# Places of the rope chain's steps, of the wide output projection, and the order of the opening in a four-layer transformer kernel

## Chip, cores, metric

One core of one Trainium2 chip. The metric is the device time of one execution in microseconds (us). The kernel before took 4762.24 us (median of 3 runs, 4760.87 to 4765.71). "TensorE" (PE, with its weight loads PEld), "VectorE" (DVE), "ScalarE" (ACT), "GpSimd" (POOL) and "SyncE" (SP, which issues the DMAs) are the five engines; each takes its instructions in order.

## The reference, cut to what matters

Four different transformer layers are applied to `x` (2 batches, 1024 tokens, 256 channels), each with modulated layer norms, self-attention, cross-attention to a context of 77 tokens and an MLP:

```python
def _rope(x, sin, cos):                 # layer 2 alone, on q and k
    xe = x[..., ::2]; xo = x[..., 1::2]
    re = xe * c - xo * s
    ro = xe * s + xo * c
...
mod = cond @ W + b                      # per layer; shifts and scales of its three norms
h = _ln(x) * (1 + scale) + shift        # layer 0 and 1: silu(cond)
q, k, v = h @ Wq, h @ Wk, h @ Wv
x = x + softmax(q @ k.T * s) @ v @ Wo + bo       # self
x = x + softmax(q @ kc.T * s) @ vc @ Wo + bo     # cross, keys and values from the context
x = x + gelu(h @ W1 + b1) @ W2 + b2
```

Layers 0 and 1 have 16 heads of 16 channels ("narrow"), layers 2 and 3 have 16 heads of 64 ("wide"). Layer 2 rotates q and k (rope), layer 3 does not; otherwise their attention is the same.

## The kernel before

The program is one list `order` of steps (L569 to L836). A `Plan` (L571) gives each step a place, a number on a scale of attention units, and sorts them; `put(lo, hi, steps)` spreads several steps evenly from lo to hi. All five engine programs (`tensor_program` L936, `scalar_program` L1306, `vector_program` L1500, `gpsimd_program` L1892, `sync_program` L1974) walk the same list and issue what the step has for them. So a step's place sets where its instructions stand in every engine's queue, and an instruction that waits on a semaphore holds up all that is behind it on its engine. Between stages there is a step "rest", a barrier of all engines. The products of TensorE go to PSUM buffers that a ring hands out in turn (`take`); a buffer is free again once its reader has signalled.

**Wide self-attention** (one stage for both batches): 32 units, each 512 queries of 2 heads against 1024 keys in 8 key tiles. For every key tile TensorE computes two scores (L948), ScalarE the exponentials (L1390), TensorE the weighted values (L1128). The row maxima for a later unit come before it: TensorE L1020, VectorE's reduction L1667 (8 per unit). GpSimd sums the probabilities of key tiles 1 to 5 (L1957, L1961), VectorE adds 6 and 7 (L1741), TensorE sums over partitions (L1138), VectorE takes reciprocals (L1756) and scales, TensorE projects (L1170), VectorE adds to x (L1777). Score banks let TensorE be two scores ahead of ScalarE's exponentials.

Every 4 units a new group g of 4 heads is prepared ("natural tiles", place o = 4g - 4 and later): weights are loaded and split, values computed (v64), and q and k each in two halves of 512 tokens (nat64). In layer 2 such a half is a **rope chain**: TensorE's projection into a pair of banks (12 matmuls, L948), ScalarE's copy (L1356), VectorE's product with cosine (L1652, frees the bank pair) and GpSimd's with sine (L1935), GpSimd's two rotations (L1941, L1942), ScalarE's copy rounded to the high part (L1362), VectorE's subtraction for the low part (L1659). It is planned in three steps, `nat64`, `rturn`, `rlow`; ScalarE's L1362 belongs to `rturn`, right behind GpSimd's rotation. Then SyncE stacks the tiles by DMA (`kstack`, `qstack`: 8 DMAs each, L2093 and L2110), for which it waits for the chain's end. Layer 3 has a copy (L1344) and a subtraction (L1639) only. The cosine product lies in the tile of the weight stage, the sine product in that of the normalised layer-norm input.

**Wide cross-attention**: 32 units with 77 keys. For each: scores twice (cs, L948), maxima (L1724), exponentials (L1411), reciprocal (L1733), GpSimd's scaling (L1948), transposes (cturn, L1052) and ScalarE's copy (L1419), weighted values (cav, L1064), ScalarE's output copy (fin, L1400), projection (proj, L1170), addition (L1777). Their places (L604 to L609) relative to the unit: -1.25, -0.85, -0.45, 0, 0.5, 0.51, 0.9.

**Opening**: the small loads and x, statistics of the first layer norm (L1543 to L1551), then `cond` for all four layers: 12, 12, 8 and 12 products of 4 matmuls with two columns (L948), ScalarE's eviction (L1316) and VectorE's combination into scale and shift (L1518 to L1527). Then the norm in four rounds: L1558, transposes L969, scale and shift L1329, split L1569 and L1571; the addition of a bias row to x (GpSimd, L1899); the split of the first weights (L1581, L1905); a barrier. The first stage then begins with the projections of batch 0 (L948), their storing and restacking by DMA, and 32 maxima (L1024, L1671) before the first scores.

## Time and profile before

| | |
|---|---|
| median of 3 runs | 4762.24 us |
| the profiled execution, its own time | 4768.35 us |
| its span, first to last instruction | 4766.6 us |
| busy share PE, DVE, ACT, POOL | 87%, 65%, 44%, 28% |
| mean granted TensorE clock | 0.935 of full |

The span is a little less than the execution's time, which is more than the median of the runs by 6 us. Places in the trace: opening 0 to 77 us, layer 2 self-attention 1771 to 2839, its cross-attention to about 3220, layer 3's self-attention to 4308, its cross-attention to about 4610. A busy share is that of an engine over all stages; a line such as `ACT x <- POOL y: us, times, longest` says how long ScalarE stood before its instructions of line x until those of line y had ended.

### The profile page before, as it was taken

What the parts mean: (1) busy time and instruction counts of PE and PEld (TensorE: products, weight loads), DVE (VectorE), ACT (ScalarE), POOL (GpSimd) and SP (SyncE); (2) the same over time, 40 slices, a digit from 0 to 9 for tenths busy, and PEclk for the clock granted to TensorE, in tenths of its full rate; (3) what the DMA queues carried; (4) which work ended last, traced back from release to release, by engine and by line L of the source; (5) the groups of instructions that cost most, each with busy time, mean ns of one, the idle gap of its engine ahead of it and who ended that gap; (6) DMA issues with size and microseconds to landing.
All of it is one profiled execution on the core that took longest, in us unless ns stands there. A gap on an engine that the chain in (4) does not pass through costs nothing. (4 is left out here: it accounts for less than half of the span.)

```text
span 4766.6 us, 56541 instructions
## 1 busy us (share of the span) xinstructions
PE 4157.7 (87%) x20828; PEld 2548.7 (53%) x20828; DVE 3079.0 (65%) x4625; ACT 2080.2 (44%) x3756; POOL 1344.8 (28%) x664
## 2 busy tenths in 40 slices
PE   6899989789998878888888876788799899997989
PEld 4343356633335665554555445567555555545768
DVE  4888855688885655667666763345477777774455
ACT  2555544355554433333333434454244444444541
POOL 1000001200001024554555553321144444451120
PEclk9999989899998988999999998889899999998999
DMA  4223231122323142222222215333223233215420
GB/s 120 29 53 47 42 56 34 45 27 52 45 42 59 32 79 65 46 52 63 56 62 62 50 29 120 80 63 73 62 61 72 54 70 76 63 39 135 104 64 18
DMA packets 158515, 286.64 MB, mean 60 GB/s; under 512 B 36458, under 2 KB 70052, under 8 KB 157216
## 3 DMA queue, kind: packets, MB, share of 16 engines
q1 hardware_dynamic: 158240, 283.03, 28.6%
q8 instruction: 166, 2.72, 0.3%
q14 instruction: 109, 0.89, 0.1%
HBM read 105.01 MB, written 29.64 MB: 28 GB/s over the span
## 5 line engine op out<-in xcount | busy, mean ns | idle before, releaser
L948 PE MATMUL PS<-t 128*128 128x512 f32 (+4 forms) x7896 | 2006.1, 386 | 224.1 <-ACT t L1390 100.9
L948 PEld LDWEIGHTS PS<-t 128*128 128x128 f32 (+2 forms) x7896 | 1258.7, 188 | 786.0 <-issue 259.5
L1390 ACT ACTIVATE t<-PS 128x512 f32<-128x512 f32 (+2 forms) x1600 | 1164.7, 750 | 1094.6 <-PE PS L948 1088.1
L1667 DVE TENSOR_REDUCE t<-PS 128x1 fp32r<-128x1024 f32 x512 | 621.9, 1220 | 311.8 <-PE PS L1020 305.6
L1128 PE MATMUL PS<-t 128*32 128x512 f32 (+2 forms) x4352 | 816.9, 615 | 0.2
L1671 DVE TENSOR_REDUCE t<-PS 128x1 f32<-128x512 f32 x1024 | 649.2, 682 | 75.5 <-PE PS L1024 74.1
L1961 POOL TENSOR_TENSOR t<-t 128x1024 f32<-128x1024 f32 x256 | 621.1, 2426 | 148.1 <-ACT t L1390 123.6
L1024 PE MATMUL PS<-t 96*128 96x512 bf16 x1024 | 374.9, 396 | 37.5 <-DVE t L1671 13.5
L1020 PE MATMUL PS<-t 128*128 128x512 f32 x1024 | 340.4, 416 | 59.2 <-DMA t<-t 26.8
L1957 POOL TENSOR_TENSOR t<-t 128x1024 f32<-128x1024 f32 x64 | 155.6, 2431 | 747.7 <-PE PS L1138 469.7
L1899 POOL TENSOR_TENSOR t<-t 128x2048 f32<-128x2048 f32 x24 | 109.6, 4569 | 899.2 <-DMA t<-in_rows 560.6
L1128 PEld LDWEIGHTS PS<-t 128*32 128x32 f32 (+2 forms) x4352 | 171.7, 122 | 331.3 <-issue 326.9
L1170 PE MATMUL PS<-t 128*128 128x256 f32 x1024 | 284.3, 427 | 69.7 <-ACT t L1400 51.1
L1024 PEld LDWEIGHTS PS<-t 96*128 96x128 bf16 x1024 | 97.0, 97 | 375.7 <-DVE t L1671 157.1
L1170 PEld LDWEIGHTS PS<-t 128*128 128x128 f32 x1024 | 211.5, 213 | 119.5 <-ACT t L1400 63.8
L1777 DVE TENSOR_TENSOR t<-PS,t 128x1024 f32<-128x1024 f32 x128 | 156.6, 1223 | 169.8 <-PE PS L1170 169.6
L1020 PEld LDWEIGHTS PS<-t 128*128 128x128 f32 x1024 | 198.0, 198 | 125.5 <-DVE t L1667 32.4
L1756 DVE RECIPROCAL PS<-PS 128x256 f32<-128x256 f32 x128 | 224.7, 1756 | 12.5 <-PE PS L1138 12.5
L1258 PE MATMUL PS<-t 128*128 128x256 f32 x1536 | 215.9, 292 | 13.4 <-DVE t L1873 4.7
L1258 PEld LDWEIGHTS PS<-t 128*128 128x128 f32 x1536 | 204.8, 197 | 26.0 <-issue 10.1
L1411 ACT ACTIVATE t<-PS,t 128x77 f32<-128x77 f32 x512 | 159.3, 324 | 105.9 <-DVE t L1724 105.8
L1873 DVE TENSOR_TENSOR t<-t 128x512 fp32r<-128x512 f32 x128 | 112.8, 882 | 128.2 <-ACT t L1493 127.0
(134 smaller groups left out, 3936.2 us busy)
## 6 DMA issues: line engine op xcount, KB each, us to landing
t<-t SPq DMA_DIRECT2D x512, 128.0 KB, 3.6
t<-t SPq DMA_DIRECT2D x256, 256.0 KB, 3.9
t<-scr_n SPq DMA_DIRECT2D x288, 128.0 KB, 6.3
scr_n<-t SPq DMA_DIRECT2D x72, 256.0 KB, 2.2
t<-t SPq DMA_DIRECT2D x256, 64.0 KB, 2.0
t<-in_L_Wg SPq DMA_DIRECT2D x16, 768.0 KB, 4.5
t<-in_L_W SPq DMA_DIRECT2D x36, 256.0 KB, 3.3
t<-in_L_Wo SPq DMA_DIRECT2D x64, 128.0 KB, 2.6
```

What stands on the lines that cost most here:

```text
L948: ins = e.matmul(out, l, r, start=i == 0, stop=i == len(terms) - 1, tile_position=tp)
L1020: ins = e.matmul(o[:, 512 * h:512 * h + 512], u.smq[j][qt], u.smk[j][h], start=True, stop=True)
L1024: e.matmul(o, u.smq[j][qt], u.smk[j][half], start=True, stop=True).then_inc(*bank_full[k].inc(nth))
L1128: ins = e.matmul(banks[S.ot][wd * j:wd * j + wd, :], u.v[j][kt], P[0:S.pr, j, :], start=kt == 0, stop=kt == S.nkt - 1, tile_position=(0, w ...
L1170: ins = e.matmul(o[:, 256 * q:256 * q + 256], S.OR[n % 2][:, 128 * q:128 * q + 128], u.wo[:, :], start=True, stop=True)
L1258: ins = e.matmul(banks[4 + q][:, 0:D], l, r, start=m == 0 and t == 0, stop=m == 7 and t == 2)
L1390: e.activation(dst, src, ACT.Exp, scale=S.L.scale).then_inc(*expd.inc((S.i, i)))
L1411: ins = e.activation(S.PQ[n % 3][:, j, t, :], o[:, 256 * t + CT * b:256 * t + CT * b + CT], ACT.Exp, bias=S.NM[n % 3][:, at], accum_out=S. ...
L1667: e.tensor_reduce(S.MT[m % 2][:, qt, j:j + 1], o, AX.X, ALU.max, negate=True).then_inc(*bank_free[k].nth(nth))
L1671: e.tensor_reduce(S.NMX[:, 4 * j + qt, half:half + 1], o, AX.X, ALU.max).then_inc(*bank_free[k].nth(nth))
L1756: e.reciprocal(o[:, hs], o[:, hs]).then_inc(*recip_made.inc((S.i, n, h)))
L1961: e.tensor_tensor(S.AP_[:, :, :], S.AP_[:, :, :], P[1][:, :, :], ALU.add).then_inc(*pool_summed.inc((S.i, n, kt)))
```

## The change

1. The rope chain is planned in five steps instead of three: `nat64` (projection, ScalarE's copy), `rcos` (cosine on VectorE, sine on GpSimd), `rturn` (rotation on GpSimd), `rhigh` (ScalarE's high copy), `rlow`. A new function `nat64_chain` gives each its own place, in layer 2's self- and cross-attention. The first groups of both stages, in the MLP before and at the start of cross-attention, keep an evenly spaced list, now of five steps.
2. In both wide cross-attentions the projection stands at 1.3 instead of 0.9.
3. Opening: layer 0's modulation weights are loaded before x; the first weights are loaded and split before the norm; only layer 0's products come before the norm, layer 1's stand three at a time between its rounds; layer 2's come after the first projections, layer 3's between the maxima, and the bias addition at -7.5. The norm waits for its own layer's modulation alone.

```diff
@@
-        Wmod = [sbt(c, [128, 2, 128 * L.nmod]) for L in Ls]
+        Wmod = [sbt(c, [128, 2, 128 * L.nmod]) for L in Ls[1:]]
         mods = [sbt(c, [128, L.nmod, NB]) for L in Ls]
+        sbt(c, [128, 120])
+        Wmod.insert(0, sbt(c, [128, 2, 128 * Ls[0].nmod]))
@@
-                             (0.9, ("proj", S, u.n, 0))):
+                             (1.3, ("proj", S, u.n, 0))):
@@
-                out += [(w, S, g, qk, half) for w in ("rturn", "rlow")]
+                out += [(w, S, g, qk, half) for w in ("rcos", "rturn", "rhigh", "rlow")]
         return out
+
+    def nat64_chain(plan, S, g, qk, at, steps):
+
+        for half in range(2):
+            for i, what in enumerate(("nat64", "rcos", "rturn", "rhigh", "rlow") if S.L.rope else ("nat64",)):
+                plan.put(at[half] + steps[i], 0, [(what, S, g, qk, half)])
@@
-    order.append(("setup",))
     first = line[0]
-    norm0 = norm_steps(first)
-    order.extend(norm0[:9])
-    order.extend(("cond", L) for L in Ls)
-    order.extend(norm0[9:])
-    order.extend(weight_steps(first))
+    order.append(("setup", 0))
+    order.append(("mod_load", Ls[0]))
+    order.append(("setup", 1))
+    order.append(("w_load", first, 0))
+    order.append(("setup", 2))
+    order.extend(("mod_load", L) for L in Ls[1:])
+    order.extend(("ln_stats", first, t) for t in range(8))
+    order.append(("ln_rstd", first))
+    order.append(("w_split", first, 0, 0))
+    order.append(("cond", Ls[0], 0, 12))
+    order.extend(("ln_norm", first, t) for t in range(4))
+    for q in range(4):
+        order.append(("ln_turn", first, q))
+        order.append(("cond", Ls[1], 3 * q, 3 * q + 3))
+        order.append(("ln_split", first, q))
+        order.extend(("ln_norm", first, t) for t in range(2 * q + 4, min(2 * q + 6, 8)))
@@
                         begin16_steps(S, plan, -20, -19, -17, -9, -8)
+                        plan.put(-16, 0, [("cond", Ls[2], 0, 8)])
+                        plan.put(-9, -8, [("cond", Ls[3], 2 * i, 2 * i + 2) for i in range(6)])
+                        plan.put(-7.5, 0, [("ln_bias", first)])
@@
-                        plan.put(o + 2.3, o + 3.7, nat64_steps(S, g, 0))
+                        if L.rope:
+                            nat64_chain(plan, S, g, 0, (o + 1.3, o + 2.9), (0, 0.15, 0.3, 0.95, 1.1))
+                        else:
+                            plan.put(o + 2.3, o + 3.7, nat64_steps(S, g, 0))
@@
                         plan.put(o - 0.9, o - 0.9, [("w_split", pg, g % 4, int(g != 4))])
+                        if L.rope:
+                            plan.put(o + (0.1 if g != 4 else 0.45), o + (0.5 if g != 4 else 0.75),
+                                     [("v64", S, g, t) for t in range(2)])
+                            late = 0 if g != 4 else 0.3
+                            for qk, at in ((1, (0.35 + late, 0.8 + late * 0.8)), (0, (1.25 + late * 0.5, 1.65 + late * 0.2))):
+                                nat64_chain(plan, S, g, qk, [o + x for x in at], (0, 0.05, 0.1, 0.3, 0.34))
+                            continue
@@
-                w.wait_ge(mod_made, "all")
+                w.wait_ge(mod_made, (p.L.i, "all"))
@@
-            elif what == "rturn":
+            elif what == "rhigh":
                 S, g, qk, half = a
@@
-            elif what == "nat64":
+            elif what == "rcos":
                 S, g, qk, half = a
@@
-                e.dma_start(cols[:, :], A["cols"]).then_inc(*setup_in[0].inc(0, 16))
-                e.dma_start(cT[:, :, :], A["cT"]).then_inc(*setup_in[1].inc(0, 16))
-                e.dma_start(ident[:, :], A["ident"]).then_inc(*setup_in[2].inc(0, 16))
-                e.dma_start(sel[:, :], A["sel"]).then_inc(*setup_in[3].inc(0, 16))
+                part, = a
...
+                if not part:
+                    e.dma_start(cT[:, :, :], A["cT"]).then_inc(*setup_in[1].inc(0, 16))
+                    e.dma_start(cols[:, :], A["cols"]).then_inc(*setup_in[0].inc(0, 16))
+                elif part == 1:
+                    for h in range(2):
+                        e.dma_start(X[:, 4 * h:4 * h + 4, :], x[:, 4 * h:4 * h + 4, :]).then_inc(*x_in[h].inc(0, 16))
+                    e.dma_start(ident[:, :], A["ident"]).then_inc(*setup_in[2].inc(0, 16))
+                else:
+                    e.dma_start(sel[:, :], A["sel"]).then_inc(*setup_in[3].inc(0, 16))
+                    for h in range(2, 4):
+                        e.dma_start(X[:, 4 * h:4 * h + 4, :], x[:, 4 * h:4 * h + 4, :]).then_inc(*x_in[h].inc(0, 16))
```

## Rows read from the trace of the kernel before

**Rows 1.** Busy time by stretch: stretch, length, PE, PEld, DVE, ACT, POOL, PEclk, DMA.

```profile
1821.16:2738.98 917.82, 806.04 (x3348) 472.63 (x3347) 618.08 (x574) 351.17 (x561) 495.86 (x227) 0.94 0.25 55
3416.44:4208.20 791.76, 762.64 (x3348) 451.47 (x3347) 570.16 (x546) 326.84 (x533) 342.25 (x143) 0.99 0.28 63
2887.68:3212.02 324.34, 253.60 (x1276) 193.43 (x1276) 129.10 (x231) 166.75 (x604) 106.19 (x70) 0.87 0.38 83
4333.68:4602.19 268.51, 238.34 (x1276) 180.67 (x1276) 115.14 (x219) 154.98 (x592) 48.25 (x34) 0.93 0.49 105
```

**Rows 2.** TensorE's waits (us, times, longest) in 1821 to 2739, then 3416 to 4208.

```profile
PE PS L948 <- ACT t L1390: 82.0, 56, 6.8
...
PE PS L948 <- ACT t L1390: 12.2, 29, 2.2
```

**Rows 3.** ScalarE's waits in 1821 to 2739.

```profile
ACT t L1362 <- POOL t L1942: 141.9, 28, 7.0
```

**Rows 4.** Timeline, one rope chain, Q (start, duration, what, idle before).

```profile
2004.90 1.03 ACT L1356 ACTIVATE t<-PS 128x1024 f32<-128x1024 f32 x1 [4.15 <-PE PS L948]
...
2005.96 1.23 DVE L1652 TENSOR_TENSOR t<-PS,t 128x1024 f32<-128x1024 f32 x1 [1.61 <-ACT t L1356]
2006.01 2.38 POOL L1935 TENSOR_TENSOR t<-t 128x1024 f32<-128x1024 f32 x1 [2.67 <-ACT t L1356]
...
2011.90 1.26 POOL L1942 TENSOR_TENSOR t<-t 128x512 f32<-128x512 f32 x1
...
2013.19 1.06 ACT L1362 ACTIVATE t<-t 128x1024 fp32r<-128x1024 f32 x1 [6.28 <-POOL t L1942]
...
2014.79 2.07 PE L948 MATMUL PS<-t 128*128 128x512 f32 x4 [2.50 <-ACT t L1390]
```

**Rows 5.** VectorE's groups in 1821 to 2739 (busy us, mean ns).

```profile
L1659 DVE TENSOR_TENSOR t<-t 128x1024 fp32r<-128x1024 f32 x28 | 48.0, 1716 | 47.0 <-ACT t L1362 47.0
```

**Rows 6.** TensorE's waits in 2870 to 3300, layer 2's cross-attention.

```profile
PE PS L1170 <- ACT t L1400: 33.5, 15, 4.7
PE PS L1052 <- POOL t L1948: 29.9, 7, 8.4
```

**Rows 7.** Timeline, an undisturbed unit of layer 2's cross-attention.

```profile
3034.19 1.04 PE L1052 MATMUL PS<-t 128*77 128x128 f32 x8
...
3036.34 1.08 PE L1064 MATMUL PS<-t 77*64 77x512 f32 x4 [0.16 <-ACT t L1419]
...
3038.87 1.22 POOL L1948 TENSOR_TENSOR t<-t 128x616 f32<-128x616 f32 x1 [5.47 <-DVE t L1733]
3039.04 1.99 PE L1170 MATMUL PS<-t 128*128 128x256 f32 x8 [0.48 <-ACT t L1400]
...
3040.87 1.04 PE L1052 MATMUL PS<-t 128*77 128x128 f32 x8
```

**Rows 8.** Timeline of the opening.

```profile
6.73 0.43 DVE L1543 BATCH_NORM_STATS2 t<-t 128x6 f32<-128x256 f32 x1 [2.75 <-DMA t<-in_x]
...
11.30 0.21 ACT L1321 ACTIVATE t<-t 128x8 f32<-128x8 f32 x1 [6.89 <-DVE t L1549]
...
14.93 37.71 PE L948 MATMUL PS<-t 128*128 128x2 f32 x176 [14.93 <-DMA t<-in_Wmod]
...
35.91 0.17 DVE L1518 TENSOR_SCALAR t<-t 128x2 f32<-128x2 f32 x1 [9.30 <-ACT t L1316]
...
39.32 0.23 DVE L1527 TENSOR_SCALAR t<-t 128x2 f32<-128x2 f32 x1
...
69.25 2.61 DVE L1569 CAST t<-t 128x512 fp32r<-128x512 f32 x1 [2.32 <-ACT t L1329]
...
72.51 0.95 DVE L1581 CAST t<-t 128x1536 fp32r<-128x1536 f32 x1
...
77.33 15.22 PE L948 MATMUL PS<-t 128*128 128x512 f32 x60 [9.23 <-POOLq L1969]
```

**Rows 9.** Timeline, the first maxima of the first stage.

```profile
106.47 18.74 PE L1024 MATMUL PS<-t 96*128 96x512 bf16 x32 [6.03 <-DMA t<-scr_n]
```

More of the change, by code:

```diff
@@ L952, in tensor_program @@
             if what == "cond":
-                L, = a
+                L, lo, hi = a
                 w.wait_ge(wmod_in[L.i], L.i)
@@ L957, in tensor_program @@
                 src = sT if L.silu else cT
-                for m in range(L.nmod):
+                for m in range(lo, hi):
                     o, k, nth = take(w, ring, ("cond", L.i, m))
@@ L1308, in scalar_program @@
             if what == "setup":
+                if a[0]:
+                    continue
                 w.wait_ge(setup_in[1], 0)
@@ L1311, in scalar_program @@
             elif what == "cond":
-                L, = a
+                L, lo, hi = a
                 w.wait_ge(setup_in[0], 0)
-                for m in range(L.nmod):
+                for m in range(lo, hi):
                     o, k, nth = full(w, ("cond", L.i, m))
@@ L1502, in vector_program @@
             if what == "setup":
+                if not a[0]:
+                    e.memset(ones[:, :], 1.0).then_inc(*set_up.inc("ones"))
+                if a[0] < 2:
+                    continue
                 w.wait_ge(setup_in[2], 0)
                 e.tensor_copy(identb[:, :], ident[:, :]).then_inc(*set_up.inc("ident"))
-                e.memset(ones[:, :], 1.0).then_inc(*set_up.inc("ones"))
             elif what == "cond":
-                L, = a
+                L, lo, hi = a
+                if hi < L.nmod:
+                    continue
                 k, nth = where["cond", L.i, L.nmod - 1]
@@ L1520, in vector_program @@
                         if aff is None:
-                            e.tensor_copy(mb, mod[:, 2 * sh + k, :]).then_inc(*mod_made.inc("all"))
+                            e.tensor_copy(mb, mod[:, 2 * sh + k, :]).then_inc(*mod_made.inc((L.i, "all")))
                         else:
@@ L1526, in vector_program @@
                             w.wait_ge(mod_made, (L.i, s, k, 1))
-                            e.tensor_scalar(ma, ma, col(aff + "_w", k), None, ALU.mult).then_inc(*mod_made.inc("all"))
+                            e.tensor_scalar(ma, ma, col(aff + "_w", k), None, ALU.mult).then_inc(*mod_made.inc((L.i, "all")))
             elif what == "ln_stats":
@@ L1924, in gpsimd_program @@
                                     ).then_inc(*nat_2.inc((S.i, ch)))
-            elif what == "nat64" and a[0].L.rope:
+            elif what == "rcos":
                 S, g, qk, half = a
@@ L1981, in sync_program @@
             if what == "setup":
-                e.dma_start(cols[:, :], A["cols"]).then_inc(*setup_in[0].inc(0, 16))
-                e.dma_start(cT[:, :, :], A["cT"]).then_inc(*setup_in[1].inc(0, 16))
-                e.dma_start(ident[:, :], A["ident"]).then_inc(*setup_in[2].inc(0, 16))
-                e.dma_start(sel[:, :], A["sel"]).then_inc(*setup_in[3].inc(0, 16))
+                part, = a
                 x = A["x"].rearrange("(t p) d -> p t d", p=128)
-                for h in range(4):
-                    e.dma_start(X[:, 4 * h:4 * h + 4, :], x[:, 4 * h:4 * h + 4, :]).then_inc(*x_in[h].inc(0, 16))
-            elif what == "cond":
+                if not part:
[9 more added lines that the diff above has]
+                        e.dma_start(X[:, 4 * h:4 * h + 4, :], x[:, 4 * h:4 * h + 4, :]).then_inc(*x_in[h].inc(0, 16))
+            elif what == "mod_load":
                 L, = a
```

## The prediction

> **What bounds the kernel now.** I read the page first, then busy time by stretch, then who waits for whom, then the timeline of single chains. The profiled execution took 4768.35 us, which is the sum's base. No engine is saturated over the whole; TensorE is nearest, so the question is where it stands still. Layer 2 and layer 3 run the same wide attention, so layer 3 serves as a yardstick. From the first partial sum of unit 0 to that of unit 28 of self-attention, both stretches hold exactly 3348 TensorE matmuls; layer 2 needs 917.8 us and layer 3 791.8 us, at mean granted clocks of 0.94 and 0.99 [rows 1]. In the cross stretch (first to last scaling of probabilities) it is 324.3 against 268.5 us for 1276 matmuls each [rows 1]. Those two differences, 126.0 and 55.8 us, are what rope costs where TensorE should hide it.
>
> The waits say how. In layer 2's self stretch TensorE's score matmuls wait 82.0 us for ScalarE's exponentials, in layer 3's 12.2 us [rows 2]. ScalarE itself waits 141.9 us, 28 times, for GpSimd's second rotation instruction (L1942) ahead of the high copy L1362 [rows 3]. The timeline of one half chain shows it [rows 4]: ScalarE's copy from PSUM at 2004.90, the sine product on GpSimd for 2.38 us, the two rotations ending at 2013.16, the high copy at 2013.19, and only at 2014.79 TensorE's next scores, 2.50 us idle. ScalarE takes work in order; with two exponentials of look-ahead, a wait of 5 to 6 us passes through to TensorE.
>
> **Rope chains in self-attention.** Nothing is added or removed: 7 groups x Q, K x 2 halves = 28 chains keep all instructions. The high copy moves from the place of the rotation (0.09 unit after the projection for K, 0.12 for Q) to 0.3 unit after it, the subtraction L1659 to 0.34; cosine, sine and rotation get places at 0.05 and 0.1. Without the excess a unit lasts 791.8 / 28 = 28.3 us, so the high copy is due 8.5 us after the projection's place instead of 3. GpSimd's part, measured from the end of ScalarE's copy, is 2.38 + 2 x 1.26 = 4.9 us, with a partial sum between (as in this timeline) 7.2 us [rows 4]. It fits, so the 141.9 us should go almost entirely. What queues behind the moved places: on VectorE the cosine product frees the PSUM pair, and at most one maximum (eight per unit, 0.125 apart) can precede it; on GpSimd the fifth partial sum of a unit now comes after sine and rotation of the last Q half, some 1.3 us late for the sum that VectorE continues; on SyncE the stacking DMAs of Q start at 2.05 units of the group, the last subtraction is at 1.99, and eight K DMAs (from 2.01) are issued before them, so they don't start later. The next weight load is at 2.5. Upper bound: layer 3's pace, 126. I leave 16 us unrecovered (28 additional high copies that scores can meet, about 0.4 us each, and the late fifth sums): **110 us**. Lower bound 60, if half the wait only changes its place.
>
> One rule speaks against the new place. The row: the subtraction L1659 averages 1.716 us over 28 [rows 5] where an undisturbed VectorE pass over as many elements takes 1.23 [rows 4]; it sits beside GpSimd additions already. Put later, it falls amid GpSimd's partial sums (as long as the sine product, 2.38) oftener. The Trainium skill (SBUF — State Buffer, Who interferes with whom) says that a VectorE instruction with two SBUF inputs and a GpSimd one that reads SBUF exclude each other, the later one waiting it out whole. The trace's longer passes agree with it. I don't take a cost for this, since VectorE is busy 618 of 918 us there [rows 1]; what it would be if all of it told is rival (a).
>
> **Rope chains in cross-attention.** Six groups (12 half chains) move, in the same way. TensorE waits 29.9 us for the scaling L1948, queued behind sine and rotations, and 33.5 us at the projection for ScalarE's output copy, queued behind the high copy [rows 6]. After: the first half has the scaling between sine and rotation. From the end of the projection matmuls: copy 1.1, sine 2.4, scaling 1.2, so the probabilities' transposes can begin at 4.7; TensorE has 2.2 us of work until then (36.34 to 39.04 without 0.48 idle [rows 7]), a wait of 2.5, of which 0.6 is in every unit already (next part): 1.9. The second half comes 1.6 units later, and costs some 0.7. That leaves 2.6 us per group where the excess over layer 3 is 55.8 / 6 = 9.3: 6.7 x 5 = 33, and for the fifth group (g = 4) I add only 2. Its first projection now stands at 8.3 units, amid the layer norm that it needs (6.75 to 9.2), and its sine must wait for the norm's last split, since both share a tile. **35 us**; bounds 0 and 56.
>
> **Output projection 0.4 unit later.** Both wide cross stages. In an undisturbed unit TensorE goes transposes 3034.19, ..., projection 3039.04 (0.48 idle), next transposes 3040.87 [rows 7]: period 6.68, of which 0.16 + 0.48 = 0.64 waiting. Moved behind the second scores, the projection no longer waits for the output copy. But VectorE's addition of its result (1.23 us) now comes before the reciprocal that the scaling needs. From the projection's start: matmuls 1.99, addition 1.23, reciprocal and hand-over 0.3 (an estimate), scaling 1.22 = 4.7 us until the next transposes. Transposes and second scores take 1.99 (34.19 to 36.34 without 0.16), so TensorE's own work in that time is 6.68 - 0.64 - 1.99 = 4.05, and the period is 1.99 + 4.7 = 6.7. The wait changes its cause: **0 us**. Bounds: the 0.48 could go in the 32 units of one stage (+16), or a layer norm's VectorE work in the same gap could add 0.65 for half of 62 units (-20).
>
> **Opening.** Now all 176 modulation matmuls run from 14.93 for 37.71 us, 0.857 per product of four [rows 8]; then four rounds of norm, transposes and split until 72.51, the weight split, the first projection at 77.33 [rows 8]. After: layer 0's 12 products come first. Its weight DMA goes ahead of the x quarters (8 tiles, two quarters, are needed). About 3.1 MB arrived between 6.73, when the first quarter was there, and 14.93, 0.38 MB/us; so the second quarter lands at 6.73 + 1.57 / 0.38 + 0.52 / 0.38 = 12.2. Statistics take 4.4 (6.73 until ScalarE's root at 11.30, less the hand-over), so the root is at 16.6. ScalarE evicts products only behind the root and three banks hold three, so nine follow: 16.6 + 9 x 0.857 = 24.3, with the vector work 25.5. The rounds took 19.9 with 1.2 of vector work; with three layer-1 products in each, and layer 1's vectors (3.6, 35.91 to 39.55) before the last split, I take 20.6 (19.9 - 1.2 + 3.6, less 1.7, since the bias addition on GpSimd no longer stretches a cast of the last round, 2.61 [rows 8]; an estimate). First projection at 46.5: 30.8 earlier. The weight split leaves the path; the bias addition on GpSimd goes beside the maxima and is due only before the first output addition. Given back: layer 2's 8 products (6.9) lie in the gap before the first maxima at 106.47, their vectors, now before VectorE's memset, cost about 2 of their 3.6. Layer 3's 12 (10.3 us) stand among 32 maxima that take 18.74, 0.59 each at VectorE's pace [rows 9]: I charge 6; bounds 0, and 20.6 if all are exposed at TensorE's lower clock level. Net **23 us**, bounds 9 and 31.
>
> Layer 1's MLP holds the first chains of layer 2, now in five evenly spaced steps: 0, up to +5.
>
> **Sum:** 110 + 35 + 0 + 23 = 168; 4768.35 - 168 = 4600. The median of the shown runs, 4762.24, is 6 below the profiled one, so the forecast for the median is **4594 us**.
>
> **Rivals** (all for the median).
> (a) GpSimd and VectorE block each other: every later subtraction meets a partial sum, is lengthened by its 2.38 us, and passes that on to TensorE through the maxima behind it; 28 x 2.38 = 66, 168 - 66 = 102 gives 4660. For: 1.716 against 1.23 [rows 4, 5]. Against: VectorE has idle time. The rule of the Trainium skill above (SBUF — State Buffer) would have it so.
> (b) Layer 2 becomes as fast as layer 3 throughout, and the opening reaches its bound: 126 + 56 + 31 + 5 = 218, 4544. Against: GpSimd still has 28 x 4.9 us more to do.
> (c) The steps don't take effect: positions differ but ScalarE still meets an unfinished rotation (GpSimd delayed by partial sums), so only the opening stays: 4739.
> (d) Slower: VectorE's queue becomes the gate. The cosine product, behind whatever VectorE has first, holds one of two PSUM pairs, and the projection's addition stands before every reciprocal. If cosine comes more than 4.5 us (126 / 28) after the copy, self-attention loses what it won: at 5.2 us, 20 slower; in cross 64 x 1.23 - 35 = 44 slower; opening 23 faster: 4803.
> (e) As (c), with the opening's gain lost to layer 3's products: 4760.
>
> **How the numbers follow.** Forecast 0.60, (a) 0.22, (b) 0.08, (c) 0.05, (d) 0.03, (e) 0.02. The forecast's own spread is about 4560 to 4640 (self 80 to 126, cross 15 to 45, opening 15 to 28); the range has to reach (a): 4555 to 4670, leaving out (c), (d), (e) and most of (b). A measurement of this kernel can tell about 0.2% (9.5 us) from no change. Faster: 0.60 + 0.22 + 0.08 + 0.05 = 0.95; same 0.02; slower 0.03.
>
> **What would show it.** In the profile after: ScalarE's wait for L1942's successor near zero; TensorE's wait for exponentials in layer 2's self stretch near 20 us, its clock near 0.99, and 28 units in about 808 us; cross 324 down to about 290, with short waits at the transposes instead of the projection; layer 3's cross unchanged at 268; first projection near 46, first maximum 23 to 30 us earlier than 106.47. The prediction is wrong if ScalarE still waits over 50 us there, if VectorE's cosine product lets TensorE wait for a bank, or if layer 3's cross moves by more than 16 us.

## The result, and the profile after

The changed kernel takes 4627.17 us (median of four runs, 4616.11 to 4631.79) against 4761.56 us of the kernel before (four runs, 4753.2 to 4765.71): ratio 0.9717, 95% interval 0.9695 to 0.9739. The forecast was 4594, with a range of 4555 to 4670. The profiled execution took 4616.11 us, the fastest of its four, so the profiles differ by 152.2 us and the medians by 134.4. What the profiles differ by can be laid out along the program, by the same instructions in both: 21.7 us in the opening, 5.8 in layers 0 and 1 up to layer 1's last transposes of maxima, -9.5 from there to layer 2's first transposes, 88.5 in the 28 units of layer 2's self-attention, 45.0 in its cross stretch, -3.8 in layer 3's cross stretch, and 4.5 in all that is left. The forecast had 23, 0, 0, 110, 35, 0, 0. (A minus sign means slower.) The 5.8 are chance: in the ten profiles taken with this opening and layer 1 unaltered, layer 1's last transposes stand anywhere from 1570.6 (this one) to 1579.9 us.

Busy time by stretch, changed kernel; columns and order as in [rows 1] (layer 2 self, layer 3 self, layer 2 cross, layer 3 cross).

```profile
1803.63:2632.98 829.35, 771.26 (x3348) 449.98 (x3347) 627.38 (x574) 352.81 (x561) 495.48 (x226) 0.99 0.28 60
3263.88:4052.61 788.73, 759.97 (x3348) 449.68 (x3347) 568.89 (x546) 326.87 (x533) 342.31 (x142) 1.00 0.28 64
2782.64:3061.95 279.31, 230.43 (x1276) 175.91 (x1276) 129.08 (x231) 165.89 (x604) 105.72 (x71) 0.94 0.44 96
4178.66:4450.99 272.33, 231.61 (x1276) 176.21 (x1276) 117.21 (x219) 154.78 (x592) 48.24 (x34) 0.95 0.48 104
```

Read the first column after the colon pair against [rows 1]: 917.8 became 829.4, 324.3 became 279.3, and layer 3's cross stretch grew from 268.5 to 272.3. In layer 2's self stretch 34.8 of the 88.5 us is shorter matmul time (806.0 to 771.3, clock 0.94 to 0.99), the rest less idle time.

Waits in that stretch of the changed kernel (us, times, longest): first ScalarE's at the high copy, which answers to [rows 3], then TensorE's, which answer to [rows 2].

```profile
ACT t L1395 <- POOL t L1980: 19.5, 23, 4.5
...
PE PS L979 <- ACT t L1423: 11.6, 21, 2.2
PE PS L979 <- DVE t L1705: 10.1, 5, 2.5
PE PS L1169 <- DVE t L1779: 8.9, 7, 1.8
PE PS L1051 <- DVE t L1690: 7.2, 5, 1.7
PE PS L1201 <- DVE t L1690: 6.4, 7, 3.5
```

ScalarE's wait fell from 141.9 to 19.5 us and TensorE's wait for exponentials from 82.0 to 11.6, about layer 3's 12.2. The next four rows all end in VectorE: maxima (L1705), the last partial sum (L1779), the cosine product (L1690) twice. They make 32.6 us. In the kernel before the same waits were:

```profile
PE PS L948 <- DVE t L1667: 11.2, 5, 2.2
...
PE PS L1170 <- DVE t L1652: 2.0, 1, 2.0
...
PE PS L1138 <- DVE t L1741: 0.5, 1, 0.5
```

That is 13.7 us. So the wait for maxima is not new (11.2, now 10.1); what grew is the last partial sum (0.5 to 8.9) and the cosine product, which frees PSUM banks (2.0 to 13.6). The prediction had named "if VectorE's cosine product lets TensorE wait for a bank" as a sign of being wrong. That sign is there, with 13.6 us of 829: rival (d)'s wait acts, but at a small part of the gain.

The opening of the changed kernel, in its timeline:

```profile
8.40 2.72 PE L979 MATMUL PS<-t 128*128 128x2 f32 x12 [8.40 <-DMA t<-in_Wmod]
...
45.21 13.98 PE L979 MATMUL PS<-t 128*128 128x512 f32 x52 [5.28 <-DVEq L1921]
...
76.13 0.65 PE L1055 MATMUL PS<-t 96*128 96x512 bf16 x1
76.58 1.71 PE L979 MATMUL PS<-t 128*128 128x2 f32 x8
78.14 2.58 PE L1055 MATMUL PS<-t 96*128 96x512 bf16 x5
80.71 1.87 PE L979 MATMUL PS<-t 128*128 128x2 f32 x8
...
105.94 0.59 PE L1116 MATMUL PS<-t 128*12 128x128 bf16 x4 [3.09 <-DVE t L1741]
```

The first projection comes at 45.21 (forecast 46.5) instead of 77.33 [rows 8], the first maximum at 76.13 instead of 106.47 [rows 9]. The maxima with layer 3's products between them then take 29.8 us to the transposes (L1116) where the 32 maxima alone took 21.2 (106.47 to 127.67): 8.6 given back, 6 forecast. The transposes stand at 105.94 instead of 127.67, so 21.7 stay.

The largest loss, 9.5 us, stands in layer 1's MLP, where the second of layer 2's four first chains looks like this in the kernel before:

```profile
1743.59 1.08 ACT L1356 ACTIVATE t<-PS 128x512 f32<-128x512 f32 x2
...
1744.71 1.29 DVE L1652 TENSOR_TENSOR t<-PS,t 128x512 f32<-128x512 f32 x2 [0.28 <-ACT t L1356]
1744.75 2.41 POOL L1935 TENSOR_TENSOR t<-t 128x1024 f32<-128x1024 f32 x1 [3.30 <-ACT t L1356]
...
1745.91 1.80 DVE L1873 TENSOR_TENSOR t<-t 128x512 fp32r<-128x512 f32 x1
...
1750.14 1.06 ACT L1362 ACTIVATE t<-t 128x1024 fp32r<-128x1024 f32 x1 [4.31 <-POOL t L1942]
```

and in the changed one:

```profile
1719.33 1.08 ACT L1389 ACTIVATE t<-PS 128x512 f32<-128x512 f32 x2
...
1720.49 3.04 POOL L1973 TENSOR_TENSOR t<-t 128x1024 f32<-128x1024 f32 x1 [3.30 <-ACT t L1389]
...
1721.61 2.48 DVE L1911 TENSOR_TENSOR t<-t 128x512 fp32r<-128x512 f32 x1 [0.31 <-ACT t L1526]
1724.01 1.27 DVE L1690 TENSOR_TENSOR t<-PS,t 128x512 f32<-128x512 f32 x2
1724.74 4.39 PE L979 MATMUL PS<-t 128*128 128x512 f32 x18 [2.17 <-DVE t L1690]
1725.41 1.29 POOL L1979 TENSOR_TENSOR t<-t 128x512 f32<-128x512 f32 x1 [1.88 <-DVE t L1690]
...
1727.99 1.06 ACT L1395 ACTIVATE t<-t 128x1024 fp32r<-128x1024 f32 x1 [6.42 <-POOL t L1980]
```

The MLP's subtraction (L1873, now L1911) needs 0.69 us alone. Beside GpSimd's sine product it takes 1.80 or 2.48, and ends some 0.6 us after that product's end in both timelines (1747.71 against 1747.16, 1724.09 against 1723.53), as if it had been held until then. In the old order the cosine product is already done by then. In the new one it stands behind the stretched subtraction, 4.7 us after the start of ScalarE's copy instead of 1.1. TensorE (2.17) and GpSimd (1.88) wait for it, and ScalarE waits 6.42 us for the rotation instead of 4.31. The four copies lie 37.8 us apart from first to last (1703.07 to 1740.84) instead of 32.4. That is rival (d)'s mechanism, in a stage where I had not looked for it. The run with old places there (below) tests it.

### The profile page after: what moved, and what is told of

Same layout as the page of the kernel before. It is cut to its first block, busy times and chain, and to the rows that moved or that the text cites. A ratio compares the mean times of both kernels' runs of the same rounds, so it can differ in the third digit from the quotient of the medians.

```text
span 4614.3 us, 56558 instructions
## 1 busy us (share of the span) xinstructions
PE 4087.4 (89%) x20828; PEld 2506.3 (54%) x20828; DVE 3092.6 (67%) x4625; ACT 2080.6 (45%) x3756; POOL 1345.0 (29%) x664
## 4 chain that ended last, share of the span: by engine, by line
PE 60%; DVE 16%; issue 6%; ACT 6%; POOL 5%; SPq 4%; DMA 3%; DVEq 0%; POOLq 0%; ACTq 0%
PE PS L979 25%; PE PS L1159 12%; PE PS L1055 4%; PE PS L1201 4%; PE PS L1051 4%; DVE t L1709 3%; PE PS L1289 3%; PE PS L1211 2%; DVE t L1705 2%; SPq L2154 2%; SPq L2137 2%; POOL t L1973 1%; DVE PS L1794 1%; POOL t L1999 1%; POOL t L1986 1%
## 5 line engine op out<-in xcount | busy, mean ns | idle before, releaser
L979 PE MATMUL PS<-t 128*128 128x512 f32 (+4 forms) x7896 | 1983.1, 382 | 153.5 <-ACT t L1423 30.6
L979 PEld LDWEIGHTS PS<-t 128*128 128x128 f32 (+2 forms) x7896 | 1242.9, 186 | 700.6 <-issue 253.1
L1705 DVE TENSOR_REDUCE t<-PS 128x1 fp32r<-128x1024 f32 x512 | 621.6, 1219 | 285.8 <-PE PS L1051 278.9
L1201 PE MATMUL PS<-t 128*128 128x256 f32 x1024 | 253.8, 392 | 28.9 <-DVE t L1690 10.2
L1051 PEld LDWEIGHTS PS<-t 128*128 128x128 f32 x1024 | 195.3, 196 | 130.8 <-DVE t L1705 36.5
L1201 PEld LDWEIGHTS PS<-t 128*128 128x128 f32 x1024 | 194.4, 196 | 66.6 <-issue 25.1
L1289 PE MATMUL PS<-t 128*128 128x256 f32 x1536 | 217.6, 294 | 11.9 <-POOL t L2005 4.7
L1289 PEld LDWEIGHTS PS<-t 128*128 128x128 f32 x1536 | 206.5, 198 | 24.4 <-issue 8.4
L1911 DVE TENSOR_TENSOR t<-t 128x512 fp32r<-128x512 f32 x128 | 114.7, 897 | 147.9 <-ACT t L1526 146.6
```

Of the source, the lines that this page charges most:

```text
L979: ins = e.matmul(out, l, r, start=i == 0, stop=i == len(terms) - 1, tile_position=tp)
L1051: ins = e.matmul(o[:, 512 * h:512 * h + 512], u.smq[j][qt], u.smk[j][h], start=True, stop=True)
L1201: ins = e.matmul(o[:, 256 * q:256 * q + 256], S.OR[n % 2][:, 128 * q:128 * q + 128], u.wo[:, :], start=True, stop=True)
L1289: ins = e.matmul(banks[4 + q][:, 0:D], l, r, start=m == 0 and t == 0, stop=m == 7 and t == 2)
L1705: e.tensor_reduce(S.MT[m % 2][:, qt, j:j + 1], o, AX.X, ALU.max, negate=True).then_inc(*bank_free[k].nth(nth))
```

## Experiments

All are edits of the changed kernel; a stretch is named as above, and a median is compared with the changed kernel's 4627.17. The kernel before was measured again beside every group of runs, with medians from 4757.76 to 4762.57, so a difference of some 5 us between medians of different groups says little. "Old places" means that cosine and sine stand at the projection and the high copy at the rotation, as before:

```
def old_put(plan, lo, hi, steps):
    groups = []
    for s in steps:
        if s[0] in ("rcos", "rhigh"):
            groups[-1].append(s)
        else:
            groups.append([s])
    for i, grp in enumerate(groups):
        at = lo + (hi - lo) * i / len(groups)
        plan.put(at, at, grp)
```

**The opening alone** (all chains at old places, projection at 0.9).

> The changed kernel with all rope chains back at their old places and the projection back at 0.9: of the change only the opening is left. Theory A (the trace's places): the first transposes of the maxima stay 21.7 us earlier than in the kernel before, every later stage has its old length (28 units of layer 2's self-attention 918 us, its cross stretch 324, layer 3's cross stretch 268.5, the last four chains before layer 2 with copies from first to fourth 32 us apart), so the whole is 22 us below the kernel before (ratio 0.995). Rival (the opening's gain came from somewhere else or is partly given back later, at layer 2's or 3's modulation): the first transposes are 21.7 earlier, but the whole is less than 12 us below.

Median 4743.14 against 4760.16 of the kernel before in the same session, ratio 0.996 (0.9938 to 0.9981): 17.0 us, with an interval of 9 to 30. In the profile the first transposes come at 105.90, the stretches are 917.5, 321.0 and 268.8, and the two profiled executions differ by 22.0 us (4746.31 against 4768.35). The profile bears out Theory A, that the opening keeps nearly what it wins; the medians alone would allow the rival too.

**Self-attention's chains at old places.**

```
-                        if L.rope:
+                        if False:
...
-                            plan.put(o + at, o + to, steps)
+                            old_put(plan, o + at, o + to, steps)
```

> The changed kernel with the chains of layer 2's self-attention (groups 1 to 7) back at their old places, all else as changed. Theory A: these places are worth 88 us, all inside that stage: 28 units take 829 + 88 = 917 us again, ScalarE's wait for the second rotation instruction is 140 us again (19.5 in the changed kernel), the whole is 88 us slower than the changed kernel, and the cross stage keeps its 279. Rival (the clock or the opening carries part of it: a busier stage gets a better clock whatever the places): 28 units take 890 or less.

Median 4712.53, 85.4 us slower. ScalarE's wait is back to the digit:

```profile
ACT t L1406 <- POOL t L1991: 141.9, 28, 6.9
```

But the stretch is 905.3 us, not 917, with the same places. Unit 4 there (first row), in the kernel before (second) and in the changed kernel (third), busy time by stretch:

```profile
1930.34:1974.36 44.02, 36.74 (x159) 23.38 (x159) 24.88 (x21) 15.77 (x25) 25.55 (x13) 0.96 0.12 25
```

```profile
1946.45:1992.84 46.39, 39.29 (x159) 25.19 (x159) 24.98 (x21) 15.78 (x25) 25.52 (x13) 0.89 0.12 25
```

```profile
1918.40:1951.93 33.53, 31.20 (x144) 19.54 (x144) 23.14 (x20) 14.71 (x23) 23.21 (x11) 1.00 0.16 34
```

TensorE stood idle 7.3 and 7.1 us in the first two; what differs between them is the granted clock, 0.96 and 0.89, and with it matmul time by 2.6 us. In the kernel before, the clock fell to its lower level after an idle time of 2.24 us (ahead of 1968.91) and again with one of 4.00 (ahead of 1981.97); in this run it stayed up after the same 2.24 and fell only after one of 4.17. So what idle time costs in clock differs from execution to execution of the same order. Over the 28 units the old order took 917.8, 917.5 and 905.3 us in three profiles, nearly all of the difference matmul time (806.0, 805.6 and 793.6); the new order took 827.2 to 833.4 in six. The places are worth 72 to 91 us by these, and 85 by the medians. Of the 75.9 us by which this profile is longer than the changed kernel's, 22.3 are matmul time.

**Only the high copy near the rotation**: `(0, 0.05, 0.1, 0.3, 0.34)` becomes `(0, 0.05, 0.1, 0.12, 0.34)`.

> The changed kernel with only the high copy of self-attention's chains put close behind the rotation again (0.12 instead of 0.3 unit after the projection); cosine, sine, rotation and subtraction keep their new places. Theory A (what gains is the distance between rotation and high copy on ScalarE's queue): ScalarE waits 100 us or more for the second rotation instruction instead of 19.5, and 28 units take 890 to 920 instead of 829. Rival (the other new places carry a good part of the 88 us): 850 to 880.

Median 4719.41, 92.2 us slower; 28 units take 925.2.

```profile
ACT t L1395 <- POOL t L1980: 117.2, 27, 6.3
...
PE PS L979 <- ACT t L1423: 83.2, 48, 5.1
```

Without the high copy's new place the other new places bring nothing: Theory A, and even 5 us beyond its range. The converse, the high copy moved alone, was not run. Nearest to it is the run with cosine and sine back at the projection (below): there cosine and sine stand as before relative to the projection, the rotation almost so (0.1 against 0.09 and 0.12), while the high copy, the subtraction and the start of each half chain keep their new places, and the stage keeps its 830 us.

What is lost here is not stretching by GpSimd: the subtractions average 1.36 us instead of 2.12, and the stage is 96 us longer all the same.

**Cross-attention's chains at old places.**

```
-                            nat64_chain(plan, S, g, 0, (o + 1.3, o + 2.9), (0, 0.15, 0.3, 0.95, 1.1))
+                        old_put(plan, o + 2.3, o + 3.7, nat64_steps(S, g, 0))
```

> The changed kernel with the chains of layer 2's cross-attention (groups 2 to 7) back at their old places, projection kept at 1.3. Theory A (chains carry the gain in cross): the stretch of 32 scalings goes from 279 to 320 or more, most of the 45 us. Theory B (the later projection carries a good part): it goes to 300 to 312, because the projection no longer waits for ScalarE's output copy behind the high copy (33.5 us of wait in the kernel before).

Median 4673.68, 46.5 us slower; the stretch takes 333.9 us: Theory A.

**The projection back at 0.9.**

```
-                             (1.3, ("proj", S, u.n, 0))):
+                             (0.9, ("proj", S, u.n, 0))):
```

> The changed kernel with the output projection back at 0.9 in both wide cross stages. Theory A (the place is neutral, as forecast): both stretches within 4 us of the changed kernel (279 and 272). Theory B (it helps beside rope chains and costs without them): layer 2's stretch 8 to 15 us longer, layer 3's 4 us shorter (268.5, as in the kernel before). Theory C (it costs in both): both shorter by 4.

The median is 4627.76. By the profile it is Theory B: layer 2's stretch takes 291.0 us, layer 3's 268.5.

These two with the opening-only run give all four corners of layer 2's cross stretch: old chains 321.0 (projection 0.9) and 333.9 (1.3); new chains 291.0 and 279.3. TensorE's largest wait in that stage with old chains and 1.3, then with new chains and 0.9:

```profile
PE PS L1091 <- POOL t L1994: 81.1, 27, 8.4
```

```profile
PE PS L1083 <- POOL t L1986: 22.2, 12, 8.4
```

The later projection costs 12.9 us where the chains are old (the wait for ScalarE's copy, 33.4, becomes one for the scaling, 29.9 to 81.1) and gives 11.7 where they are new. All four are single profiles. With new chains and 1.3 ten profiles have 279.2 to 284.2, so the gain is 7 to 12 us; with old chains and 0.9 there is also the kernel before with 324.3, so the cost is 10 to 13. The sign of each is clear, the size is not. Of the 11.7, 8.5 lie in the stretch's first ten units (116.2 against 107.7), where a layer norm runs beside them; the reason I can't show. In layer 3 it costs: 266.7 to 268.8 in the five profiles with 0.9, 271.8 to 278.3 in the nine with 1.3. At the median nothing is left of it. Of the stretch's 45 us, the chains alone are 30, both together 42.

**The MLP's four chains at old places**: `old_put(plan, 24.6, 28.6, ...)` and `old_put(plan, 28.6, 32.6, ...)`.

> The changed kernel with the four first chains of layer 2, those in layer 1's MLP, back at their old places. The stretch from the last transposes of layer 1's maxima to the first of layer 2's takes 200.5 us in the kernel before and 210.0 in the changed one. Theory A (in the changed order VectorE's square subtraction meets GpSimd's sine product, is stretched from 0.69 to 2.48 us, and puts the cosine product, and with it the PSUM bank and the rotations, 2 us later, four times): 200 to 202 again, first to fourth copy 32 us apart instead of 37.8. Rival (the stretch is longer because the clock happened to be lower in it, 0.86 against 0.89): 206 or more.

From layer 1's last transposes (1577.64) to layer 2's first (1778.92) 201.3 us, the copies 32.3 apart from first to fourth: Theory A. The other profiles agree, so it is not the rival's chance of the clock: this stretch takes 207.1 to 210.0 us in the nine profiles with the new places and 199.8 to 201.6 in the five with the old ones, 7.7 us less in the mean. Median 4612.7, ratio to the kernel before 0.9696 (0.9681 to 0.971): 14.5 us faster than the change as it was made, of which the stage explains 8 to 9; the rest is scatter. The subtraction is still stretched there, now behind the cosine product:

```profile
1725.04 1.29 DVE L1701 TENSOR_TENSOR t<-PS,t 128x512 f32<-128x512 f32 x2 [0.28 <-ACT t L1400]
1725.09 2.40 POOL L1984 TENSOR_TENSOR t<-t 128x1024 f32<-128x1024 f32 x1 [3.30 <-ACT t L1400]
1726.25 1.79 DVE L1922 TENSOR_TENSOR t<-t 128x512 fp32r<-128x512 f32 x1
```

**What is left of layer 2's excess over layer 3** (829.35 - 788.73 = 40.6 us; 29.3 of it is idle time of TensorE, 11.3 longer matmul time) was tried in three ways. The rope subtraction of the changed kernel had become slower again, where [rows 5] have 1716 ns; below its group in the 28 units, and one of the long ones in the timeline:

```profile
L1697 DVE TENSOR_TENSOR t<-t 128x1024 fp32r<-128x1024 f32 x28 | 59.4, 2122 | 3.6 <-ACT t L1395 3.6
```

```profile
2047.48 8.18 POOL L1999 TENSOR_TENSOR t<-t 128x1024 f32<-128x1024 f32 x3
...
2050.20 3.25 DVE L1697 TENSOR_TENSOR t<-t 128x1024 fp32r<-128x1024 f32 x1
...
2053.98 1.20 DVE L1705 TENSOR_REDUCE t<-PS 128x1 fp32r<-128x1024 f32 x1
...
2055.23 3.95 PE L979 MATMUL PS<-t 128*128 128x512 f32 x16 [2.50 <-DVE t L1705]
```

Three partial sums on GpSimd, the subtraction amid them for 3.25 us, the maximum behind it late, TensorE idle 2.50. That looked like the cause, as rival (a) had it. The trace also has its size: all five waits of the score matmuls for maxima (10.1 us) stand behind a subtraction that took 2.05 to 3.26 us, and in the kernel before all five (11.2 us) behind one of 2.28 or 2.29. So the stretched subtraction does reach TensorE, with some 10 us, but as much before the change as after it.

> The changed kernel with the subtraction that makes the low part computed on GpSimd instead of VectorE, in self-attention (28 times). On VectorE it averages 2.12 us, either 1.22 (where GpSimd is idle) or 3.2 to 3.4 (amid partial sums). Theory A (these stretched subtractions delay maxima and last sums, and are most of the 40.6 us that layer 2 needs more than layer 3): VectorE busy falls by 55 to 60 us in the 28 units and they take 800 to 815 instead of 829. Rival (VectorE has room, 627 of 829; GpSimd then gets 28 x 2.4 = 67 us more, and its partial sums come later): 829 to 850.

The edit moves self-attention's `rlow` from VectorE's program to GpSimd's, under a semaphore of its own (the four in layer 1's MLP go with it):

```
+            elif what == "rlow":
...
+                w.wait_ge(nat_high, (S.i, i))
+                e.tensor_tensor(T[:, 2:4, ts], S.TE, f(T[:, 0:2, ts]), ALU.subtract).then_inc(*nat_lowp.inc((S.i, i)))
```

28 units take 847.6, the median is 4645.42, 18.3 slower. VectorE now waits for GpSimd (the next cosine product for the subtraction, first row, and the last sums for GpSimd's partial sums, second):

```profile
DVE t L1691 <- POOL t L1991: 28.6, 8, 4.6
DVE t L1782 <- POOL t L2010: 23.9, 7, 4.0
```

The score matmuls' waits for maxima are gone; TensorE's wait for the last sum rose from 8.9 to 20.1. But this run doesn't end the overlap of the two engines, it moves it. VectorE's own partial sums, which also read two tiles in SBUF, are the ones stretched now; their group in the changed kernel (first) and in this run (second):

```profile
L1779 DVE TENSOR_TENSOR t<-t 128x1024 f32<-128x1024 f32 x56 | 72.1, 1288 | 18.1 <-POOL t L1999 18.1
```

```profile
L1782 DVE TENSOR_TENSOR t<-t 128x1024 f32<-128x1024 f32 x56 | 88.4, 1578 | 23.9 <-POOL t L2010 23.9
```

So VectorE was relieved of 39.6 us (627.4 to 587.8), not of the 55 to 60 expected, and what the stage would take without any such stretching stays open.

> The changed kernel with cosine and sine product of self-attention's chains directly at the projection (0 instead of 0.05 unit after it; the second Q half of group 4 stands 0.06 unit later so that the order stays possible). Theory A (what is left of layer 2's excess comes from VectorE giving the PSUM pair free late, TensorE waits 13.6 us for the cosine): those waits fall to under 5 us and 28 units take 815 to 822 instead of 829. Rival (the maximum that now stands behind the cosine is late instead, or the exclusion sets the pace): 829 within 4.

Steps `(0, 0, 0.1, 0.3, 0.34)`: 830.1 us, median 4626.22. The stretch is as long as before, the rival's number, but not by its mechanism. Of the 13.6 us of waits for the cosine 0.5 is left, and the waits for maxima fell too (10.1 to 6.8), as did the stretching (the subtractions take 47.0 us instead of 59.4). What rose is ScalarE's wait at the high copy, from 19.5 to 58.0 us, and with it TensorE's wait for exponentials, from 11.6 to 22.5:

```profile
ACT t L1395 <- POOL t L1980: 58.0, 26, 4.5
```

So ScalarE's wait over 50 us, one of the prediction's signs of being wrong, says little alone: here it costs TensorE only 11 us more.

> The changed kernel with four instead of five partial sums on GpSimd, and three instead of two on VectorE, in the first two of every four units of layer 2's self-attention up to unit 27 (14 units), which hold the rope chains. Theory A (what is left of layer 2's excess over layer 3, 40.6 us, comes from GpSimd: it is late with the fifth sum behind two sine products and four rotations, VectorE waits for it 18.1 us and the maxima behind it are late): 28 units take 800 to 815 instead of 829. Rival (VectorE, which gets 14 x 1.25 = 17.5 us more, sets the pace of these units, by exclusion or by its own work): 829 to 845.

```
+    def pool_parts(S, n):
+        return 4 if S.L.rope and n < 28 and n % 4 in (0, 1) else 5
...
-                if 1 <= kt < 6:
+                if 1 <= kt < pool_parts(S, n) + 1:
...
```

823.6 us and a median of 4617.72 (ratio 0.9696, 0.9676 to 0.9715): 5.8 and 9.5 us better, between the ranges of Theory A and of its rival. The six profiles with five sums and the same places have 827.2 to 833.4, so the gain of the stage is outside their scatter, by 3.6 us at least. VectorE's wait for the partial sum is gone:

```profile
DVE t L1782 <- POOL t L2002: 0.6, 1, 0.6
```

and so is TensorE's for the last sum (8.9), but the 8.5 + 8.5 + 6.4 us of waits for maxima and cosine stay. So the late fifth sum was a part. That VectorE's queue, which got 15 us more, is the other is argued from these waits and not shown: no run relieved VectorE without loading GpSimd. Some 35 us of excess over layer 3 remain (823.6 against 789.1 in the same profile), whose cause stays open.

**Layer 3's modulation products ahead of the maxima**: `plan.put(-15.9, 0, [("cond", Ls[3], 0, 12)])`.

> The changed kernel with all twelve modulation products of layer 3 ahead of the first maxima, behind layer 2's, instead of in pairs between the maxima. Theory A: the stretch from the first maximum to the transposes shrinks from 29.8 to 21.2 us, and since TensorE stands idle 7.2 us ahead of the first maximum and needs 0.45 us for a product there, the first maximum comes only 1 us later: transposes at 98 instead of 105.9. Rival (TensorE at its lower clock needs 0.86 us each, and VectorE's memset and additions come 5 us later): transposes at 102 to 103.

```profile
60.91 16.82 PE L979 MATMUL PS<-t 128*128 128x2 f32 x90 [0.91 <-DVE t L1660]
79.84 0.97 PE L979 MATMUL PS<-t 128*128 128x256 f32 x6 [2.11 <-DVE t L1668]
80.66 18.62 PE L1055 MATMUL PS<-t 96*128 96x512 bf16 x32
101.74 0.59 PE L1116 MATMUL PS<-t 128*12 128x128 bf16 x4 [2.46 <-DVE t L1741]
```

The transposes come 4.2 us earlier (101.74), where the rival had 102 to 103 and Theory A 98: the products take 0.86 us each again and put the first maximum 4.5 us later, which leaves 4.2 of the 8.6 us won back at the maxima. Median 4621.63.

**The repairs together.**

> The changed kernel with the three parts put right that the runs showed as losses: the four chains in layer 1's MLP at their old places, layer 3's modulation products all ahead of the first maxima, and the projection at 0.9 in layer 3 (1.3 stays in layer 2, where the chains are). By the stretches of the earlier profiles 6 to 9, 4 and 4 to 6 us: 14 to 19 us less than the changed kernel, median 4608 to 4613. Rival (the run with the MLP's chains alone gave 14.5 us at the median, more than its stretch; so part of it was chance, and the three together give 10 or less): 4617 or more.

The edits are those of the MLP's chains and of layer 3's products, and `(1.3 if S.L.rope else 0.9, ("proj", S, u.n, 0))`.

Median 4607.18, ratio 0.9676 (0.966 to 0.9693): 20.0 us below the changed kernel, as Theory A had it and a little more. Layer 3's cross stretch is 268.5 again.

> The three repaired parts of the run before (median 4607.18) together with four instead of five partial sums on GpSimd in the 14 units with rope chains, which alone took 5.8 us off the 28 units and 9.5 off the median. Theory A (the gains lie in different stages and add up): 5 to 9 us below that run, median 4598 to 4602, 28 units in 820 to 824. Rival (with the MLP's chains repaired the first group starts in another phase of the clock, and the rest is within the scatter of the runs): 4605 or more.

Median 4602.63 over five runs, ratio 0.9669 (0.9653 to 0.9684), the fastest of all: 24.5 us below the changed kernel. 28 units take 823.4. Over the run before it is 4.6 us, just below what Theory A asked, and within what runs of one kernel differ by.

## Why the prediction was right, and where not

The median lies midway between the forecast's 4594 and rival (a)'s 4660, inside the range; the runs say that the forecast's mechanism is the one that acts, and that what it fell short by is not the 66 us of (a). Rivals (b) to (e) fall as wholes; (d)'s wait for the cosine product acts in two places, with 13.6 us in self-attention and some 8 in the MLP. Step by step:

- **Self-attention, 110 forecast: 85 by the median, 88.5 and 75.9 by the profiles.** The gain hangs on the distance of the high copy from the rotation (ScalarE's wait 141.9 to 19.5; with the high copy alone moved back, all is lost). The term was too large by some 25 us. The step that failed is "I leave 16 us unrecovered": what is left is 40.6. I had named both items, late fifth sums and high copies among scores, but priced them from ScalarE's side. TensorE's wait for exponentials did fall to layer 3's 12; what I did not price was TensorE's waits for VectorE (32.6 us, of which 18.9 are new), and that matmul time stays 11.3 us above layer 3's. The last sum is 8.9 of them, the one part that a run took away.
- **The exclusion of VectorE and GpSimd, rival (a), 0.22.** The trace shows it plainly: the subtraction takes either 1.22 us or, 13 times of 28, about 2.3 in the kernel before and mostly 3.2 to 3.4 in the changed one, while the cosine product, which has one input in PSUM, keeps 1.22 throughout. That agrees with the Trainium skill (SBUF — State Buffer, Who interferes with whom), by which a VectorE instruction with two inputs in SBUF contends with a GpSimd instruction that reads SBUF, and one with at most one such input, outside VectorE's 2-port modes, does not. As a forecast of the time it was too strong: the stretching grew by 11.4 us (48.0 to 59.4), not 66, and what of it reaches TensorE through the maxima, some 10 us, is no more than before. Taking the subtraction off VectorE lost 18 us, but it stretched VectorE's partial sums instead, so it is no test of a kernel without the exclusion. What a stretched instruction costs is decided by what is queued behind it. In the MLP that was the cosine product, and there it cost 7 to 10 us.
- **Layer 1's MLP, "0, up to +5": -9.5 in this profile, -7.7 in the mean of all.** The wrong step is that evenly spaced steps would be neutral. The rival that I had bound to self-attention (cosine late behind VectorE's first work) happened here, and the run with old places shows it.
- **Cross-attention, 35: 42 to 45.** Right in kind: the wait of 33.5 at the projection is gone, short waits at the transposes came (41.8 in all). The chains alone, with the projection at 0.9, give 30, 5 less than the 35; what lies above it came with the later projection, which I had put at 0. What the sum left out is the clock: 16.3 of the 31.0 us won in the last 21 units (202.6 to 171.6) are shorter matmul time (163.3 to 147.0, clock 0.88 to 0.99).
- **Projection, 0 within -20 to +16.** At the median 0.6. Beneath that it is not zero but a sum of opposites, +7 to +12 in layer 2 and -3.3 to -9.8 in layer 3; I had taken one undisturbed unit for both stages and missed that its price depends on the chains beside it.
- **Opening, 23: 21.7 by the profile, 17.0 at the median.** The first projection came 1.3 us from the forecast, the first maximum 30.3 us earlier where 23 to 30 was given; layer 3's products cost 8.6 instead of 6. Two figures of that part are wrong without harm: its terms add up to 46.1 and not 46.5, and the bound of 20.6 doubles a product's 0.857 us for the lower clock, though a product took the same 0.86 at 76.58 of the changed kernel, where the recorded clock is 0.50. The bound should be 10.3; 8.6 is inside it.
- **Against the medians** 134.4 is measured where 168 was forecast. The single changes of median add up: opening 17.0, self 85.4, cross chains 46.5, projection 0.6, MLP -14.5, together 135.0. That they meet 134.4 so closely is luck: each is uncertain by several us (the MLP's is 14.5 where its stage has 8 to 9), and each was taken back alone, so that what chains and projection do for each other (24.6 us in layer 2's cross stretch: 12.9 and 11.7) is counted in both.

## What to carry to other kernels

Where an engine that takes its work in order stands still for a helper on another engine, first move the instruction that waits, by the helper's length as the timeline shows it; here the stage's 85 us were lost with the place of that one copy, and the chain's other places brought nothing without it. Then look at the engine that is next in line, in every stage where the same steps are placed, since places that suit one stage put a product that frees PSUM behind a long instruction in another. Judge parts of a change by the length of their stage in the profile and by the median of several runs together: a stage of one order varied by 12 us from profile to profile, nearly all of it matmul time at another granted clock. And when an instruction is moved to another engine to end an overlap, look whether another instruction has taken its place in it.

## What the runs showed of the hardware

- A VectorE subtraction with both inputs in SBUF (128x1024) took 1.22 us when GpSimd was idle or, which I had overlooked, began its addition later, and when one of GpSimd's additions was under way 2.27 to 2.29 us in the kernel before and 2.05 to 3.43 in the changed one (13 of 28 in each, eleven of them over 3.2 in the changed one). A product with an input in PSUM stayed at 1.22 us. It also goes the other way: an addition of GpSimd that began 0.53 us after such a subtraction (2014.28 in the kernel before) took 2.94 us instead of 2.38.
- TensorE's idle time is often paid twice, once more through its clock, though not each time (2.24 us of idle time in unit 4 were followed by the lower level in one of two profiles of one order). Unit 4 of the kernel before had 7.1 us of idle time and a clock of 0.89, its counterpart in the changed kernel 2.3 us and 1.00: of 12.9 us difference, 8.1 is matmul time. Part of that is work that moved to the next unit (159 and 144 matmuls), but over 28 units with the same 3348 matmuls it is 34.8 of 88.5 us, or 22.3 of 75.9 against the other profile of the old places.
